# GpSimd adds each chunk of probabilities in two 400-column instructions instead of one of 800

## The reference

```python
qh, kh, vh = heads(layernorm(x) @ Wq), heads(ctx @ Wk), heads(ctx @ Wv)
attn = softmax(qh @ kh.T / 8)                 # over 1444 context rows
x = x + tanh(g_xattn) * (merge(attn @ vh) @ Wo + bo)
h = silu(fp4_linear(z, w_gate)) * fp4_linear(z, w_up)    # z = layernorm(x)
x = x + tanh(g_ffn) * fp4_linear(h, w_down)
```

## Time and profile before

| what | value |
|---|---|
| time, median of 3 runs | 607.21 us (606.7 to 607.94) |
| profiled execution, span from first to last instruction | 611.0 us |
| PE busy | 559.4 us, 92% |
| DVE busy | 470.2 us, 77% |
| ACT busy | 297.9 us, 49% |
| POOL busy | 276.4 us, 45%, 234 instructions |
| POOL L505, all 95 adds | 79 + 16 instructions, 156.3 + 30.2 us |
| mean granted TensorE clock | 0.959 of full speed |

### The profile page before, as it was taken

The page is one execution under the profiler, slowest core; times in us unless marked ns, Lnnn a source line. Parts: engine busy times, 40 slices in busy tenths (PEclk is TensorE's granted clock), DMA queues, the critical chain, the costliest instruction groups (busy, mean ns, idle before and its releaser), DMA issues.

```text
span 611.0 us, 10089 instructions
## 1 busy us (share of the span) xinstructions
PE 559.4 (92%) x2969; PEld 355.6 (58%) x2969; DVE 470.2 (77%) x793; ACT 297.9 (49%) x693; POOL 276.4 (45%) x234
## 2 busy tenths in 40 slices
PE   5988999999999997999999997999999999999742
PEld 4754665666575755666566664657566665646331
DVE  2769866789877994689967996779976998687655
ACT  3434645565456543465446643465455644546211
POOL 3027253644728271372826264282736265366500
PEclk9989999999999997999999999999999999999775
DMA  9400000200020000200030000200011000000000
GB/s 172 79 1 1 1 1 1 51 1 1 5 52 2 1 1 13 50 2 1 1 56 2 1 0 13 49 2 1 1 38 20 2 0 5 1 0 1 1 4 4
DMA packets 27922, 9.71 MB, mean 16 GB/s; under 512 B 24016, under 2 KB 27600, under 8 KB 27856
## 3 DMA queue, kind: packets, MB, share of 16 engines
q1 hardware_dynamic: 27856, 8.92, 7.6%
HBM read 8.50 MB, written 0.41 MB: 15 GB/s over the span
## 4 chain that ended last, share of the span: by engine, by line
PE 73%; DVE 21%; issue 3%; ACT 1%; DMA 1%; POOL 0%; SPq 0%; POOLq 0%; DVEq 0%; ACTq 0%
PE attn L788 21%; PE scores L774 14%; PE ring L727 10%; PE scores L775 9%; DVE max L894 6%; PE ring L706 5%; PE ring L734 4%; PE ring L741 3%; DVE f_abs L362 2%; DVE rsum L901 2%; DVE f_abs L364 2%; DVE e_gate L859 2%; PE ring L747 2%; PE ring L713 1%; DVE h_fp L366 1%
## 5 line engine op out<-in xcount | busy, mean ns | idle before, releaser
L633 ACT ACTIVATE probs<-scores 120x400 f32<-120x400 f32 (+1 forms) x384 | 190.0, 504 | 238.5 <-PE scores L775 236.7
L894 DVE TENSOR_REDUCE max<-ring 116x1 f32<-116x482 f32 (+1 forms) x336 | 205.0, 648 | 39.3 <-PE ring L727 36.8
L505 POOL TENSOR_TENSOR acc_p<-acc_p,probs 120x800 f32<-120x800 f32 x79 | 156.3, 1978 | 66.4 <-ACT probs L633 62.8
L788 PE MATMUL attn<-probs,ctx_n 120*64 120x400 f32 (+1 forms) x768 | 174.5, 534 | 0.0
L774 PE MATMUL scores<-q_hh,k_hl 128*120 128x400 f32 (+1 forms) x384 | 154.4, 402 | 6.2 <-issue 5.1
L774 PEld LDWEIGHTS scores<-q_hh,k_hl 128*120 128x120 f32 (+1 forms) x384 | 70.8, 184 | 132.1 <-ACT probs L633 70.3
L775 PE MATMUL scores<-q_ls,k_h 71*120 71x400 f32 (+1 forms) x384 | 134.7, 351 | 0.0
L727 PE MATMUL ring<-k_hl,q_hh 128*116 128x482 f32 (+1 forms) x336 | 121.6, 414 | 6.2 <-DVE max L894 5.7
L775 PEld LDWEIGHTS scores<-q_ls,k_h 71*120 71x120 f32 (+1 forms) x384 | 71.6, 186 | 4.2
L727 PEld LDWEIGHTS ring<-k_hl,q_hh 128*116 128x116 f32 (+1 forms) x336 | 58.9, 181 | 15.1 <-DVE max L894 7.7
L788 PEld LDWEIGHTS attn<-probs,ctx_n 120*64 120x64 f32 (+1 forms) x768 | 38.4, 136 | 47.4 <-issue 35.2
(11 more groups left out here) (126 smaller groups left out, 514.3 us busy)
## 6 DMA issues: line engine op xcount, KB each, us to landing
ctx_n<-in_ctx SPq DMA_DIRECT2D x16, 360.0 KB
wq<-in_L_xattn_Wq SPq DMA_DIRECT2D x1, 512.0 KB, 4.7
wo<-in_L_xattn_Wo SPq DMA_DIRECT2D x1, 512.0 KB, 7.6
x_in<-in_x SPq DMA_DIRECT2D x8, 50.0 KB
out<-y_out SPq DMA_DIRECT2D x8, 50.0 KB
wk<-in_L_xattn_Wk SPq DMA_DIRECT2D x1, 256.0 KB, 4.0
ctx_n<-in_ctx SPq DMA_DIRECT2D x16, 1.0 KB
wv<-in_L_xattn_Wv SPq DMA_DIRECT2D x1, 256.0 KB, 6.4
```

The source lines that it names most:

```text
L505: pool.tensor_tensor(acc_p[0:r, t.g % 2, :], left, probs[0:r, c % PROBS, :], ALU.add).then_inc(sum_p, 1)
L633: act.activation(probs[0:r, c % PROBS, k * HALF:(k + 1) * HALF], scores[0:r, slot % SCORE_BANKS, 0:HALF], ACT.Exp).then_inc(probs_full, 1)
L788: mm = pe.matmul(attn[64 * i:64 * i + C, k, 0:HALF], ctx_n[0:r, par, c, 0, :], probs[0:r, c % PROBS, k * HALF:(k + 1) * HALF], start=(j == ...
L894: dve.tensor_reduce(max3[0:rows, tile, part:part + 1], src[0:rows, 0:MAXC[part + 1] - MAXC[part]], AX.X, ALU.max).then_inc(free, 1)
```

## The change

Each of GpSimd's adds becomes two, one for each half of the rows. The first waits only for the exponential of the first half of its chunk. Each half of an accumulator waits for the same half of the add before it, so the second half of one chunk and the first half of the next no longer wait for the instruction right before them. Each instruction counts one on `sum_p`, so whoever waits for `sum_p` waits for twice the count: the waits of VectorE and ScalarE still ask for both halves.

```diff
         def own_adds(t, which):
             own = len(chunks_of(t.g - 1)[which]) - 1
-            return t.count((ADDS_V, ADDS_P)[which], own - (ADDS_V, ADDS_P)[which])
+            return t.count((ADDS_V, 2 * ADDS_P)[which], (own - ADDS_V, 2 * (own - ADDS_P))[which])

         def added(t, c, back=0):
             by_v, by_p = chunks_of(t.g - back)
-            own, per, done = (by_v, ADDS_V, sum_v) if c in by_v else (by_p, ADDS_P, sum_p)
-            return done, t.count(per, max(own.index(c), 1) - per * back)
+            own, per, done = (by_v, ADDS_V, sum_v) if c in by_v else (by_p, 2 * ADDS_P, sum_p)
+            return done, t.count(per, (1 if c in by_v else 2) * max(own.index(c), 1) - per * back)
...
                 i, r = own.index(c), CROWS[c]
-                pool.wait_ge(probs_full, t.count(SLOTS, 2 * c + 2))
-                if i == 1:
-                    if t.g >= 2:
-                        pool.wait_ge(sum_v, t.count(ADDS_V, -ADDS_V))
-                    left = probs[0:r, own[0], :]
-                else:
-                    pool.wait_ge(sum_p, t.count(ADDS_P, i - 1))
-                    left = acc_p[0:r, t.g % 2, :]
-                pool.tensor_tensor(acc_p[0:r, t.g % 2, :], left, probs[0:r, c % PROBS, :], ALU.add).then_inc(sum_p, 1)
+                for k in range(2):
+                    rows = slice(k * HALF, (k + 1) * HALF)
+                    pool.wait_ge(probs_full, t.count(SLOTS, 2 * c + k + 1))
+                    if i == 1:
+                        if t.g >= 2 and k == 0:
+                            pool.wait_ge(sum_v, t.count(ADDS_V, -ADDS_V))
+                        left = probs[0:r, own[0], rows]
+                    else:
+                        pool.wait_ge(sum_p, t.count(2 * ADDS_P, 2 * (i - 2) + k + 1))
+                        left = acc_p[0:r, t.g % 2, rows]
+                    pool.tensor_tensor(acc_p[0:r, t.g % 2, rows], left, probs[0:r, c % PROBS, rows], ALU.add).then_inc(sum_p, 1)
```

## The result

The changed kernel takes 656.02 us (652.13 to 659.59) against 607.58 us: 1.0762 times as long, 95% interval 1.069 to 1.0833. The forecast was 597.4 us, and the range, 588.5 to 613, doesn't hold it.

The account below looks back on a forecast made before the run. TensorE was taken to bound the kernel, stalled by VectorE in odd groups. The span, 611.0 - 3.8 (loop) - 3.5 (group 15) - 2.5 (clock) = 601.2 us, gave -9.8 us: 607.2 to 597.4 us, range 588.5 to 613.

Parts of the forecast that it names:

- What bounds, and who blocks whom: TensorE waits for VectorE in odd groups; VectorE instructions with two SBUF inputs stand until the running GpSimd instruction has read.
- Stall b: TensorE's wait for `h_fp` at L751 in odd groups, 1.10 us by the record; forecast to grow by 0.2 us.
- Stall a: TensorE's wait for the maxima at L727 in odd groups; L901 ends earlier behind a half, gaining 0.84 us a group.
- the first rival: VectorE never gets in between halves that follow without a gap: +2.8 us an odd group, 626 us; chance 0.20.
- the clock in group 15: Full clock instead of 1.2 GHz behind group 15's shortened stand: 2.5 us gained, bounds 0 and 3.9.
- the walk: Step-by-step timing of VectorE's links L356 to L366 against GpSimd's head sum and halves in an odd group; `h_fp` 0.2 us later.
- the loop: The six odd groups 3 to 13, each -0.64 us net, together -3.8 us.
- Group 15: Group without maxima, where TensorE stands 4.86 us; `h_fp` forecast 3.5 us earlier, -6.0 us with the clock.
- L356 wins over the head sum: L356 starts ahead of GpSimd's first head sum, so stall b goes: -1.94 us an odd group, 589.6 us; chance 0.17.

Follow-up runs that it names:

- chained kernel: The changed kernel, halves and early start kept, but every half also waits for the one right in front of it: 599.77 us, 0.9827 of the kernel before.

## Why the prediction was wrong

**What bounds, and who blocks whom: right.** The stalls, the instructions that stand still and the fixed time after the end of a GpSimd instruction all came back in the runs. The cost of a half was right (1.05 us forecast, 1.04 measured), and so was that ScalarE wouldn't wait for GpSimd: its waits in the changed kernel name only TensorE.

**The step that failed** is the one under "Stall b" and "Stall a" which takes for granted that VectorE gets in behind the running half. In these runs it holds where the next GpSimd instruction waits for the one in front, or works on fewer partitions. The change took the wait away: a half waits for the half before the last. This was the first rival, given 0.20 against 0.47. The prediction held two places of the earlier trace rows against each other and let the more frequent one (six groups) win. It should have asked in what they differ: the frequent one was a boundary from 120 to 100 partitions, the rare one from 100 to 120. The halves all have the same partitions, and with equal partitions nothing is let in.

**The rival's price was too low as well**: 2.8 us for an odd group, 7.2 measured in group 7 (35.38 to 42.62) and 7.5 on average. By its own terms, 4 less 0.84, it should have said 3.2. The longest wait of TensorE in the group went from 1.10 to 5.23 us, 4.1 more, which is what the rival said before it took off 0.84 for stall a. That gain didn't exist, because L903 was shut out too. The rest, some 3 us, fits the fall of the clock: 6.8 us at 0.50 are worth at most 3.4 us. The prediction priced the clock in group 15 and forgot it in the rival.

**With the pause put back, the number came out, in part by luck.** The chained kernel takes 599.8 us against the forecast 597.4, and the walk's steps held: L356 behind the head sum was to lose 0.9 us more (measured 1.59 us in place of 0.62), L364 to end 1.3 us after L362 (294.85 - 293.56 = 1.3), L366 2.3 us after L364 (297.23 - 294.85 = 2.4), stall b to grow by 0.2 us a group (TensorE's recorded wait for `h_fp` from 6.6 to 8.0 us in six):

```profile
PE ring L754 <- DVE h_fp L366: 8.0, 6, 1.4
```

The waits for the maxima left that list, as forecast for stall a. But the loop was to gain 3.8 us, and its six odd groups take 6.0 us more in the profiles (224.3 against 218.3). Groups 3 and 11 gain 0.64 us each, just as forecast; groups 7 and 13 lose 2.5 each, with the granted clock at 0.50 for 6.8 us after the longer stall b. Group 3 and group 7 of the chained kernel, and the stretch after the stall in group 7:

```profile
129.37:164.16 34.79, 33.40 (x184) 21.08 (x183) 30.70 (x47) 17.68 (x42) 18.86 (x19) 1.00 0.01 3
...
268.08:305.92 37.84, 36.46 (x184) 22.56 (x183) 30.68 (x47) 17.79 (x42) 18.85 (x19) 0.91 0.01 3
...
297.60:304.40 6.80, 6.80 (x25) 3.69 (x23) 3.12 (x6) 1.99 (x5) 1.55 (x2) 0.50 0.01 2
```

The prediction had taken 0.2 us more in stall b as 0.2 us and no more. Why the clock falls in groups 7 and 13 and not in 3 and 11, behind the same wait of 1.35 us, stays open. Group 15 gave 8.3 us (63.65 to 55.38 in the profiles) where 6.0 with its clock were expected. The remaining 8.7 us between the two profiles lie at the start and in the groups outside this sum, mostly 0 and 6; some 3.5 of them are only the choice of execution, as the span before lies 3.8 us above the median of its runs and the chained kernel's 0.3. So the terms missed in both directions, and the errors cancelled in the sum.

**"L356 wins over the head sum"** (589.6 us) was right as a mechanism and nearly as a price: with the pause and chunk 4 late the time is 586.9 us, and an odd group such as 7 takes 33.2 us, 2.15 less than before, where 1.94 were said. It didn't happen by itself.

## What to carry to other kernels

Before splitting a GpSimd instruction, look at what each piece waits for. Where VectorE works on SBUF operands beside it, a wait of a piece for the piece in front may not be waste: here it was the moment in which VectorE got its turn, and looser dependencies can cost more than the split gives. With the wait kept, two pieces were worth 1.7% here, and 4% once a single early add no longer let another GpSimd instruction go ahead of a critical VectorE one; four pieces gave less than two. And price the granted clock behind a stall together with the stall: in the chained kernel a stall 0.25 us longer was followed, in two of the groups, by a fall of the clock that made them 2.5 us longer each.

## What the runs showed of the hardware

A stream of GpSimd instructions without waits among them, all on 120 partitions, kept a VectorE instruction of 0.33 us standing for 6.95 us (seven halves), and for 5.18 us with three whole adds. The Trainium skill ("SBUF — State Buffer", section "Who interferes with whom") says that the other engine blocks for the whole instruction; here it was the whole stream. A wait for completion between two instructions, which leaves 0.08 us in the trace, ends the stream; a memset that reads nothing doesn't (7.77 us). The runs don't tell whether it is the completion or the idle 0.08 us that counts. A step down from 120 to 100 partitions lets VectorE in as well (1.03 and 1.04 us), a step up doesn't (1.60 us). The Trainium skill ("GPSIMD Engine Reference", section 2.1) says that the cores of GpSimd go on to the next instruction each by itself; that would fit, if the ports are held as long as any core is at work, and a core without partitions in the next instruction changes something about it, but no run here shows single cores, so the reason stays open.
